# Cross attention on one core: when the softmax is divided, and which engine applies the layer norms

## The reference

```python
x = norm(x + gamma1 * norm(yo) + beta1)          # yo: what the bidirectional Mamba made
q, k, v = x @ w_q, ctx @ w_k, ctx @ w_v          # per head
s = q @ k.T / 8;  s[masked] = -1e30
p = softmax(s)                                   # exp(s - max) / sum
att = (p @ v) @ w_o + b_o + ctx
x = norm(x + gamma * (att - mean) / (std + 1e-3) + beta)
```

## Time and profile before

| | |
|---|---|
| median of 3 runs | 2802.37 us |
| the profiled execution's own time | 2800.31 us |
| its span (first to last instruction) | 2798.5 us |
| mean granted TensorE clock | 0.959 |
| busy over the span | PE 89%, PEld 54%, DVE 63%, ACT 48%, POOL 41% |
| the loop, 1023 to 1581 us | PE 492 of 558 us busy |

### The profile page before, as it was taken

One profiled execution on the slowest core, in us unless ns is written; L12 is line 12 of the kernel. 1 busy time (PEld: TensorE's weight loads), 2 busy tenths in 40 slices (PEclk: granted clock), 3 DMA queues, 4 the chain that ended last, 5 costly groups with the idle time before them and its releaser, 6 DMA issues. The chain is left out here.

```text
span 2798.5 us, 47512 instructions
## 1 busy us (share of the span) xinstructions
PE 2495.3 (89%) x18594; PEld 1497.2 (54%) x18594; DVE 1757.8 (63%) x3458; ACT 1353.4 (48%) x2380; POOL 1151.2 (41%) x612
## 2 busy tenths in 40 slices
PE   5999989999997778999998799999989898788899
PEld 2334434344343334544444588999845455566557
DVE  3899889989999657777767630111335667466433
ACT  4566665665664246666665321111256766222231
POOL 2788889889889613333333201222110000200030
PEclk8999999999999999999999899999989999999999
DMA  5031130321212153343334153555220000200020
GB/s 217 1 128 61 60 136 2 120 88 49 121 51 116 28 156 70 81 100 81 85 78 115 32 189 133 182 177 186 87 74 1 1 1 2 91 9 1 1 107 31
DMA packets 126094, 227.22 MB, mean 81 GB/s; under 512 B 7888, under 2 KB 97488, under 8 KB 109744
## 3 DMA queue, kind: packets, MB, share of 16 engines
q1 hardware_dynamic: 122128, 213.95, 23.5%
q0 software_dynamic: 3744, 10.23, 1.0%
HBM read 201.74 MB, written 22.41 MB: 80 GB/s over the span
## 5 line engine op out<-in xcount | busy, mean ns | idle before, releaser
L208 POOL TENSOR_TENSOR m_h<-m_h,m_bc 128x1024 f32<-128x1024 f32 x256 | 612.3, 2411 | 81.1 <-DVE m_h L521 81.1
L521 DVE TENSOR_TENSOR_SCAN m_h<-m_da,m_h 128x1024 f32<-128x1024 f32 x256 | 578.7, 2278 | 39.8 <-ACT m_da L411 39.8
L281 PE MATMUL m_psy<-m_h,m_ident 128*128 128x512 f32 x1024 | 494.0, 615 | 23.2 <-POOL m_h L208 23.2
L411 ACT ACTIVATE m_da<-x_rows,m_a_neg 128x511 f32<-128x511 f32 x512 | 330.7, 680 | 157.7 <-DVE m_h L521 154.4
L941 POOL TENSOR_SCALAR c_pr<-c_pr,c_share 128x512 f32<-128x512 f32 x128 | 200.4, 1565 | 391.2 <-DVE c_share L1239 391.2
L281 PEld LDWEIGHTS m_psy<-m_h,m_ident 128*128 128x128 f32 x1024 | 196.3, 196 | 288.4 <-issue 233.7
L508 DVE TENSOR_TENSOR m_h<-m_dtx,m_bc 128x1024 f32<-128x1024 f32 x192 | 232.3, 1210 | 28.8 <-PE m_psy L281 22.8
L1001 PEld LDWEIGHTS c_psO<-c_pT,c_vr 32*64 32x64 f32 x8192 | 131.0, 137 | 133.3 <-issue 130.5
L1001 PE MATMUL c_psO<-c_pT,c_vr 32*64 32x128 f32 x8192 | 162.8, 289 | 33.4 <-ACT c_oT L1132 28.8
L227 PE MATMUL m_rot<-early_ctx,early_w 128*128 128x512 f32 x240 | 126.6, 653 | 71.0 <-ACT m_gz L387 52.1
L1119 ACT ACTIVATE c_pr<-c_pr,c_low 128x512 f32<-128x512 f32 x256 | 180.9, 707 | 2.9 <-DVE c_low L1231 2.7
(11 more groups left out here) (378 smaller groups left out, 4051.0 us busy)
## 6 DMA issues: line engine op xcount, KB each, us to landing
m_bc<-bc_dram SPq DMA_DIRECT2D x32, 2048.0 KB, 7.5
e_up<-in_up SPq DMA_DIRECT2D x39, 1024.0 KB
c_vr<-v_dram SPq DMA_DIRECT2D x128, 256.0 KB
v_dram<-c_stage SPq DMA_DIRECT2D x32, 256.0 KB, 2.1
e_down<-in_down SPq DMA_DIRECT2D x8, 1024.0 KB
e_down<-y_dram SPq DMA_DIRECT2D x8, 512.0 KB, 7.4
h_w<-in_w SPq DMA_DIRECT2D x2, 2048.0 KB, 14.4
m_taps<-in_taps SPq DMA_DIRECT2D x1, 2560.0 KB, 12.2
```

Source lines behind the costliest of these rows:

```text
L208: pool.tensor_tensor(hq, hq, bc[:, 1, NP * s:NP * (s + 1), :], ALU.mult).then_inc(p_ready, 1)
L281: mm = pe.matmul(bank, ident[:], h[:, n % HB, e, :], start=False, stop=(s == NG - 1 and e == NP - 1))
L411: ins = act.activation(da[:, n % 2, e, at:at + L - 1], dt[:, u, j, at:at + L - 1], ACT.Exp, scale=a_neg[:, u, j, NP * s + e:NP * s + e + 1])
L521: dve.tensor_tensor_scan(flat, decay, flat, 0.0, ALU.mult, ALU.add).then_inc(scanned, 1)
```

## The change

Four things are done together in `cross_attention_stage`.

1. The probabilities are no longer divided by their row sums: POOL's `scale` (128 instructions at L941) and ACT's `scale` (128 at L1125) are gone, with their semaphores. `turn` waits for the exponentials only. The reciprocals are kept for 9 steps instead of 3.
2. Instead the outputs are multiplied. For each head pair p, at the head of PE's step n = 4p + 8, `turn_share` makes 8 matmuls of the reciprocals (broadcast over 64 columns, as weights) with the identity. They write a 128x512 map of reciprocals into `psX`: rows 0 to 63 for the first head, 64 to 127 for the second. At the head of DVE's step n, `share_out` multiplies `oT` of the pair by it. `psX` is the bank of the extras, so `turn_share` waits until the extra of the step before has been copied out, and the next extra waits for `share_out`.
3. The norms' long passes inside the loop go from DVE to POOL. DVE keeps the statistics and the small reciprocals. The places of the last norm move: its statistics from u = 19 to 16, its inversion from u = 23 to 18, its root on ACT from u = 21 to 17.
4. POOL's addition of the bias row is no longer in step 24: it stands behind the norm passes of its batch. Work before and behind the loop stays on DVE.

```diff
+                for b in range(NB):
+                    if b + 1 < NB:
+                        before(b + 1)
+                    if b >= 1:
+                        behind(b - 1)
+                    pool.wait_ge(res_loaded, 16 * b + 16)
...
+                    pool.tensor_tensor(res[:], res[:], wide(rows[:, 0:1, :]), ALU.add).then_inc(res_ready, 1)
...
+                def turn_share(p):
+                    n = LT * p + 2 * LT
+                    pe.wait_ge(x_free, sum(k < n for k in numbers))
+                    if p >= 1:
+                        pe.wait_ge(o_shared, p)
+                    pe.wait_ge(share_ready, LT * (p + 1))
+                    for t in range(LT):
+                        for i in range(2):
+                            mm = pe.matmul(psX[HD * i:HD * (i + 1), t * P:(t + 1) * P],
+                                           share[:, (LT * p + t) % 9, i:i + 1].broadcast_to([P, HD]), ident[:], start=True, stop=True)
+                    mm.then_inc(share_full, 1)
...
                     if r >= 1:
                         pe.wait_ge(x_free, r)
+                    if n >= 2 * LT:
+                        pe.wait_ge(o_shared, n // LT - 1)
...
-                            pe.wait_ge(o_kept, NM * b)
+                            pe.wait_ge(o_shared, NM * b)
...
+                    if n >= 2 * LT and n % LT == 0:
+                        turn_share(n // LT - 2)
...
-                def scale(n):
-                    act.wait_ge(share_ready, n + 1)
-                    s = pr[:, n % 3, 1, :]
-                    act.activation(s, s, ACT.Copy, scale=share[:, n % 3, 1:2]).then_inc(p_scaled[1], 1)
...
-                        dve.wait_ge(p_scaled[i], n + 1)
+                        dve.wait_ge(p_ready, 2 * n + i + 1)
                         dve.transpose(pT[:, p % 2, i, t, :], pr[:, n % 3, i, :]).then_inc(turned, 1)
+                def share_out(p):
+                    dve.wait_ge(o_kept, p + 1)
+                    dve.wait_ge(share_full, p + 1)
+                    dve.tensor_tensor(oT[:, p % NM, :], oT[:, p % NM, :], psX[:], ALU.mult).then_inc(o_shared, 1)
...
-                before_parts = {0: yo_stats, 2: yo_apply, 3: yo_scale, 4: yo_shift, 5: yo_add, 6: x_stats, 9: x_apply}
-                behind_parts = {19: next_stats, 23: next_apply}
-                norm_parts = {8: statistics, 11: normalise, 13: scale, 15: shift, 17: add_to_x}
...
+                before_parts = {0: yo_stats, 2: lambda b: invert_n("yo", b), 6: x_stats, 8: lambda b: invert_n("x", b)}
+                behind_parts = {16: next_stats, 18: lambda b: invert_n("next", b)}
+                norm_parts = {8: statistics, 10: invert_std}
```

More of the change, by code:

```diff
@@ L784, in cross_attention_stage @@
         share_ready = sem("share_ready")
-        p_scaled = [sem(f"p_scaled{i}") for i in range(2)]
+        share_full = sem("share_full")
         turned = sem("turned")
@@ L936, in _ @@
                 pool.memset(eps[:], 1e-5).then_inc(eps_ready, 1)
-                def scale(n):
[L939 to L949, removed]
+                steps = [0]
@@ new lines, in link, with apply @@
+                def link(ins):
+                    steps[0] += 1
+                    ins.then_inc(pool_step, 1)
+                    pool.wait_ge(pool_step, steps[0])
+                batch = lambda b: x[:, LT * b:LT * (b + 1), :]
+                wide = lambda a: a.broadcast_to([P, LT, D])
+                def apply(rows, mean, inverse):
+                    for t in range(LT):
+                        ins = pool.tensor_scalar(rows[:, t, :], rows[:, t, :], mean[:, t, 0:1], inverse[:, t:t + 1],
+                                                 ALU.subtract, ALU.mult)
+                        if t == LT - 1:
+                            return ins
+                        ins.then_inc(pool_step, 1)
+                        steps[0] += 1
@@ new lines, in before @@
+                def before(b):
+                    pool.wait_ge(n_ready, norm_no["yo", b] + 1)
+                    link(apply(yo, n_mv, n_std))
+                    link(pool.tensor_tensor(yo[:], yo[:], wide(gb[:, 0:1, :]), ALU.mult))
+                    link(pool.tensor_tensor(yo[:], yo[:], wide(gb[:, 1:2, :]), ALU.add))
+                    pool.wait_ge(x_loaded[1], 16 * (NB - 1))
+                    link(pool.tensor_tensor(batch(b), batch(b), yo[:], ALU.add))
+                    pool.nop().then_inc(yo_added, 1)
+                    pool.wait_ge(n_ready, norm_no["x", b] + 1)
+                    link(apply(batch(b), n_mv, n_std))
+                    pool.nop().then_inc(before_ready, 1)
@@ new lines, in behind @@
+                def behind(b):
+                    pool.wait_ge(r_ready, b + 1)
+                    link(apply(res, mv, std))
+                    link(pool.tensor_tensor(res[:], res[:], wide(rows[:, 1:2, :]), ALU.mult))
+                    link(pool.tensor_tensor(res[:], res[:], wide(rows[:, 2:3, :]), ALU.add))
+                    link(pool.tensor_tensor(batch(b), batch(b), res[:], ALU.add))
+                    pool.nop().then_inc(added, 1)
+                    pool.wait_ge(n_ready, norm_no["next", b] + 1)
+                    link(apply(batch(b), n_mv, n_std))
+                    pool.nop().then_inc(behind_ready, 1)
@@ L1060, in _ @@
                     scores(n)
-                for n in range(TOTAL + 8):
+                for n in range(TOTAL + 2 * LT):
                     b, u = divmod(n, UNITS)
+                    if n >= 2 * LT and n % LT == 0:
+                        turn_share(n // LT - 2)
                     if n + 2 < TOTAL:
@@ L1069, in _ @@
                         extra(n)
-                pe.wait_ge(o_kept, NB * NM)
+                pe.wait_ge(o_shared, NB * NM)
                 pe.wait_ge(s_read, 2 * TOTAL)
@@ L1204, in _ @@
                         root(b - 1)
-                    if 1 <= b < NB and u == 21:
+                    if 1 <= b < NB and u == 17:
                         norm_root("next", b - 1)
@@ L1343, in next_stats @@
                 def next_stats(b):
+                    dve.wait_ge(before_ready, min(b + 3, NB))
+                    dve.wait_ge(added, b + 1)
                     norm_stats(batch(b), "next", b)
@@ L1363, in _ @@
                     b, u = divmod(n, UNITS)
+                    if n >= 2 * LT and n % LT == 0:
+                        share_out(n // LT - 2)
                     if n + 2 < TOTAL:
@@ L1384, in _ @@
                     link(dve.bn_stats(stat[:, t, :], res[:, t, :]))
-                for part in norm_parts.values():
-                    part(NB - 1)
-                for part in behind_parts.values():
+                for part in last_parts:
                     part(NB - 1)
```

45 lines of the change are left out of this document (26 added, 19 removed).

## The result

The changed kernel takes 2816.46 us (median of 15 runs), the kernel before 2805.89 us (15 runs): a ratio of 1.0033, with a 95% interval of 1.0024 to 1.0042. That is slower by 0.33%, more than the 0.2% that a measurement can tell. The profiled execution took 2816.46 us, its span 2814.7 us: 16.2 us above that of before.

What follows compares the result with a forecast made beforehand. PE's own work sets the pace in 84 of 128 steps. Windows of 558.1 against 545.1 give +13.0, the end -0.5: profiled 2800.3 becomes 2812.8, the median 2 us above, so 2814 us; range 2796 to 2833.

Steps and rivals of the forecast that it cites:

- Pool's passes: Norm passes on POOL: 10.4 us up to the addition, fitting its places; only batch 0 feels two-operation passes costing double.
- step 12: A boundary between pairs in batch 0, outside the 22 full ones: pays 0.9 us.
- The boundary in a full step: Between pairs where PE is full: 0.75 us wait plus 1.2 of matmuls, 1.95; 22 of them, 42.9 us.
- rival 2: At the spread matmuls: the two column halves do not overlap, 1.9 us each, 15 more, 2829; chance 0.11.
- The boundaries behind transposes: Pair boundaries whose step before ends in transposes: four counted among the 22 at 1.95 us each, without a separate price.
- The Trainium skill on the tiling mode: At the spread matmuls: a mode change drains TensorE, a toll of at most about 0.15 us, 3 us over 22.
- The plain steps: Steps without an extra, paced by DVE: the spread falls into PE's waiting, `share_out` costs about 0.7 us at 8 boundaries.
- The wait at `o_kept` in plain steps: PE's wait once per pair, 2.29 us before, shrinks to about 0.9 without the scaling.
- The windows: The loop's four batches: 129.0, 151.2, 152.0 and 125.9 us, together 558.1 against 545.1.
- Rival 3: POOL's chains become late: transposes some 3 us late in three batches, 3 at the behind norm, 2826; chance 0.06.
- The end of the loop: Last transposes 1.7 us earlier, the last pair's spread and `share_out` cost about 1.2: -0.5 us.
- Rival 1: Plain stretches give back more than full ones pay: cheaper spread and halved kept losses, 2793; chance 0.16.

Runs made afterwards that it cites:

- e8: The changed kernel without spread matmuls and multiplication (no division), the norms' long passes back on DVE at their old steps: 2773.27 us, ratio 0.9881.
- e1: The changed kernel without the spread matmuls and without the multiplication, so the division is left out: 2762.61 us, ratio 0.9843.
- e9: The changed kernel with every wait of `turn_share` kept but none of its matmuls, and no multiplication: 2790.72 us, ratio 0.9950.
- e7: The changed kernel with all waits and spread matmuls but without the multiplication, so the division is left out: 2818.72 us, ratio 1.0043.
- e6: The kernel before, with Pool's addition to the residual rows at step 26 of a batch instead of 24: 2801.08 us, ratio 0.9986.

## Why the prediction was right, and where its terms were off

The medians are 2816 against 2814 foretold, slower as foretold. The ledger of the experiments, in us: the scaling's removal with the three meetings -32.5 (e8), Pool's passes -10.7 (e8 to e1), the waits +28.1 (e1 to e9), the matmuls +28.0 (e9 to e7), the multiplication -2.3, which is none (e7). As differences along one chain they must sum to the +10.6 of the medians. The loop's windows give -31.9, -9.8, +28.8, +24.0 and -1.3 in the same order, 9.8 together. The prediction reached +12.5 for its profiled execution, where 16.2 were measured. In the loop it had costs of 47.3 (boundaries 42.9, `share_out` 3.5, step 12 0.9) and gains of 34.4, +13.0; measured were 51.5 and 41.7, +9.8. Both were too small, and the end made up the difference.

- **The boundary in a full step: right.** Foretold 0.75 us of wait and 1.2 of matmuls, 1.95; measured a wait of 0.69 behind ACT's copy and 1.09 for the group (1.02 to the next start), 1.78 in all. The depth of eight matmuls in two tiles gave the price; the serial 1.9 of rival 2 did not come. It holds at 18 of the 22 boundaries that the prediction counted, whose steps are 31.7 us longer than in e1, 1.76 each.
- **The boundaries behind transposes: cost too low.** The other four (n = 44, 64, 76, 96), and n = 12, to which the prediction gave 0.9, have waits of 1.72 to 1.79 us; at three of the five PE then ran at the lower clock. Their steps are 19.3 us longer than in e1, 14.8 for the four. So the 22 steps cost 46.5 us, not 42.9.
- **The Trainium skill on the tiling mode** (TensorEngine Tiling, Key Properties) names a drain at a change of mode. Doubling the matmuls without one more change added 0.87, the first set with its changes 0.94 by the table above, but 1.02 from its start to that of the scores (e9's wait was 0.78 us, 0.09 longer). A toll for the changes is thus 0.07 to 0.15 us at most, within the 0.15 that the prediction allowed; that there is one was not shown.
- **The plain steps: size near, cause right only beside the multiplication.** `share_out` was to cost 0.7 at each of 8 plain boundaries. A boundary there costs 0.80 (3.43 against 2.63), but e7 shows 0.59 of it without the multiplication. A pair's boundary in batch 3 after:

```profile
1560.46 1.09 PE L1057 MATMUL carried<-c_ident,c_share 128*64 128x128 f32 x16
...
1561.48 1.13 PE L1029 MATMUL c_psS<-c_kT,c_qT 64*128 64x512 f32 x4
...
1562.36 0.56 ACT L1183 COPY c_oT<-c_psO 128x512 f32<-128x512 f32 x1
...
1562.95 0.69 DVE L1297 TENSOR_TENSOR c_oT<-c_oT,carried 128x512 f32<-128x512 f32 x1 [0.23 <-ACT c_oT L1183]
1563.06 1.20 PE L1043 MATMUL c_psO<-c_pT,c_vr 32*64 32x128 f32 x64 [0.45 <-ACT c_oT L1183]
```

  The scores end at 1562.61, DVE waits for ACT's copy until 1562.95, multiplies until 1563.64, and the next row maximum comes right behind (1563.57). So in the changed kernel DVE's chain sets this step, as foretold, and the spread lies beside it. But it lies beside it only just: without the multiplication the scores are 0.59 us late (e7). "In plain steps the spread falls into time in which PE waits for DVE anyway" holds only as long as the multiplication is there.
- **The wait at `o_kept` in plain steps: direction right, size low.** It was to fall from 2.29 to about 0.9 us and is 0.45 here, and the `attend` behind it takes 1.20 instead of 2.02 us. The granted clock of batch 3 rose from 0.92 to 0.97, which is nearer the full 2.4 GHz; of batch 0 it stayed at 0.91.
- **The windows.** Foretold 129.0, 151.2, 152.0 and 125.9; measured 128.4, 152.3, 151.9 and 122.3. Batch 3 alone misses by more than 1.1, by 3.6. The losses that would remain were overstated: without `share_out` and step 12 the prediction's list gives back 34.4 us, and the windows of e1, which has neither spread nor `share_out`, are 41.7 shorter than those of before.
- **Pool's passes.** The `tensor_scalar` of 128x256 with two operations was taken at 0.8 us, half of Pool's 128x512 with one, with twice that as the bound; it takes 1.22. In batch 0 this is felt, as the prediction said of the bound:

```profile
1048.07 2.37 POOL L967 TENSOR_TENSOR x_rows<-x_rows,c_yo 128x1024 f32<-128x1024 f32 x1
```

```profile
1050.51 1.81 DVE L1351 BATCH_NORM_STATS2 c_stat<-x_rows 128x6 f32<-128x256 f32 x4 [1.13 <-POOLq L968]
```

  DVE waits 1.13 us for Pool, and the scores after it 2.94 for DVE. Rival 3, in which this happens in every batch, did not come.
- **The end of the loop: wrong.** Foretold -0.5 us, measured +4.6 to the output projection and +1.8 behind it. After:

```profile
1586.21 1.09 PE L1057 MATMUL carried<-c_ident,c_share 128*64 128x128 f32 x16 [0.68 <-ACT x_cols L1197]
1587.23 2.09 PE L1043 MATMUL c_psO<-c_pT,c_vr 32*64 32x128 f32 x129
1590.04 2.08 PE L1043 MATMUL c_psO<-c_pT,c_vr 32*64 32x128 f32 x127 [0.71 <-issue]
1593.35 1.09 PE L1057 MATMUL carried<-c_ident,c_share 128*64 128x128 f32 x16 [1.23 <-issue]
1595.29 12.31 PE L1133 MATMUL c_psS<-c_wo,c_oT 128*128 128x256 f32 x48 [0.85 <-DVE c_oT L1297]
```

  Two groups stand there, not one, the second with 1.23 us ahead of it and a wait for the multiplication behind it. The first 48 products of the output projection then took 12.31 us; before they took 10.63, behind a wait of 0.67. In their first 3.4 us the granted clock was 0.51 after and 1.00 before, which is the 1.7 us behind the projection's start. In e1 the stretch to the projection takes 14.9 us, in before 13.2: of the 4.6, 2.9 are the spread's, and the other 1.7 come without it, and without Pool's passes too (15.0 in e8). In all three, PE pauses at one place in `attend` 2.4 to 2.8 us where before it paused 1.36, and the granted clock up to the second transposes was 0.80 in e1 and after, 1.00 before. What ends the pause the profile does not show; that cause stays open.

The terms that failed are thus the tail, by 6.9 us, the boundaries behind transposes, by 3.6 in the 22 and 3.6 in step 12, and the gains, by 7.3 in the other direction. Rival 1 came as far as that (e1 shows larger gains than were listed) and was paid back by the boundaries behind transposes. That the median is within 3 us of the forecast is partly luck of signs; the full boundary, the largest term, was not.

## What to carry to other kernels

Work added to a full engine costs its duration plus the wait at the place where it is put: half of the cost here was a wait for a copy, and moving the group behind the scores, where the copy is covered, turned +0.33% into -0.39% with the same instructions. Before moving elementwise work onto matmuls, write down for the step that sets the pace which bank each product needs and when it is free, and count the last pair as well as the steady state. Work removed from an engine that is half idle is worth something where a short instruction that others wait for stands behind it in the queue: some 28 us here, in a run in which TensorE's waiting for ScalarE's copy of the outputs fell by 19. And a wait has a second price where the clock falls behind it: look at the longest waits first, here those behind transposes.

## What the runs showed of the hardware

- Normalising passes of VectorE (128x256, two operations) beside Pool's addition on 128x1024 took 3.74 us for four; two steps apart from it they took 1.83 us (e6). Row maxima and transposes of VectorE beside that same addition kept their durations (0.69 and 0.67 to 0.69 us in e6), so it is this pair of forms, not any two. In the earlier trace rows Pool's addition ran from 1549.21 to 1551.59. VectorE's first pass, begun before it, took 0.49 us; the second, begun at 1549.42, took 2.32 us and ended at 1551.74, 0.15 us behind Pool; the last two took 0.41 each. Pool's addition kept its length (2.38 against 2.37 us). So VectorE stood still while Pool held on. The Trainium skill, SBUF — State Buffer, section Who interferes with whom, says that the two share one pair of ports, that a `tensor_scalar` can use it in its two-port modes, and that whoever issues first has it for the whole instruction while the other is blocked. The numbers agree.
- Pool's `tensor_scalar` on 128x256 took 1.22 us with two operations; with one operation on 128x512 it took 1.565.
- Eight matmuls with 128 columns into two column halves of 64 took 1.09 us, sixteen 1.97, at a granted clock of 1.00; at 0.50 and 0.57, behind waits of 1.72 and 1.78 us, eight took 1.97 and 1.74.
- The first products of the output projection ran at a granted clock of 0.51 for 3.4 us, behind idle stretches of 1.23 and 0.85 us with a group of 1.09 us between them; before, behind one of 0.67, at 1.00.
